# The sort's column one-hots in two-byte form, with their numbers laid down in pairs

## The reference, cut to what matters

```python
h = relu(layernorm(x))
support = h @ weight
h1 = segment_sum(edge_weight[:, None] * support[dst], src)   # sums over the edges, by src
h2 = segment_sum(edge_weight[:, None] * h1[dst], src)        # the same again
x = x + relu(hop_w[0] * h1 + hop_w[1] * h2 + h)
h = relu(layernorm(x))
agg = segment_sum(h[src], dst)                               # sums by dst
x = x + mlp((1 + eps) * h + agg)                             # 4 layers, batch norm and elu between
```

## Time and profile before

| | |
|---|---|
| median of 3 runs | 4513.52 us (4511.48 to 4515.73) |
| the profiled execution: time | 4512.35 us |
| the profiled execution: span of its instructions | 4510.5 us |
| start and end of the move (first L1313, end of the last L1826) | 251.04 and 495.62 us |
| PE busy in the span | 3317.1 us (74%) |
| POOL busy in the span | 2678.9 us (59%) |
| DVE busy in the span | 1936.4 us (43%) |
| ACT busy in the span | 796.7 us (18%) |

### The profile page before, as it was taken

The page is one execution under the profiler, slowest core; times in us unless marked ns, Lnnn a source line. Parts: engine busy times, 40 slices in busy tenths (PEclk is TensorE's granted clock), DMA queues, the critical chain, the costliest instruction groups (busy, mean ns, idle before and its releaser), DMA issues. The chain is left out here.

```text
span 4510.5 us, 50631 instructions
## 1 busy us (share of the span) xinstructions
PE 3317.1 (74%) x15857; PEld 2707.2 (60%) x15857; DVE 1936.4 (43%) x4586; ACT 796.7 (18%) x1968; POOL 2678.9 (59%) x2705
## 2 busy tenths in 40 slices
PE   6759677777777767777777774566666665998998
PEld 5158555555555556665665564555555555887887
DVE  7989533333333323333333331222222224556765
ACT  4059300000000000000000000000000001545656
POOL 0068677777777767777777775777777775001000
PEclk9679899999999999999999997788888887999999
DMA  4000133333333343333333334433333333223313
GB/s 140 1 2 6 51 110 109 110 114 109 109 109 113 109 95 109 110 110 113 110 110 109 112 109 115 134 105 104 105 105 104 105 105 89 94 93 127 101 60 114
DMA packets 187133, 443.82 MB, mean 98 GB/s; under 512 B 49102, under 2 KB 96514, under 8 KB 180714
## 3 DMA queue, kind: packets, MB, share of 16 engines
q0 software_dynamic: 126464, 336.63, 26.0%
q1 hardware_dynamic: 60501, 105.26, 6.8%
HBM read 382.22 MB, written 59.49 MB: 98 GB/s over the span
## 5 line engine op out<-in xcount | busy, mean ns | idle before, releaser
L1859 PE MATMUL ps<-work 128*128 128x256 f32 x6912 | 1624.9, 389 | 574.5 <-DMA work<-table_hop,idx 574.5
L771 POOL DMA_INDIRECT work<-table_hop,idx x1728 | 1651.5, 956 | 556.6 <-issue 521.8
L1859 PEld LDWEIGHTS ps<-work 128*128 128x128 f32 x6912 | 1295.6, 192 | 901.9 <-DMA work<-table_hop,idx 486.6
L816 POOL DMA_INDIRECT work<-table_gin,idx x832 | 790.8, 950 | 282.3 <-issue 228.3
L1934 PE MATMUL ps<-work 128*128 128x128 f32 x3328 | 574.0, 344 | 409.1 <-DMA work<-table_gin,idx 378.0
L1934 PEld LDWEIGHTS ps<-work 128*128 128x128 f32 x3328 | 528.5, 250 | 479.0 <-DMA work<-table_gin,idx 314.3
L1399 DVE TENSOR_SCALAR work<-iota,w_hi,edge_buf 128x256 f32<-128x256 bf16 x1728 | 580.8, 408 | 18.7 <-issue 17.5
L1512 DVE TENSOR_TENSOR sum_b<-sum_b,ps 128x256 f32 x104 | 43.9, 422 | 800.3 <-PE ps L1934 800.3
L922 ACT COPY idx<-w 128x8 int32 (+1 forms) x216 | 42.1, 197 | 1947.7 <-PE ps L1859 1907.1
L1411 DVE TENSOR_TENSOR sum_b<-sum_b,ps 128x512 f32 x108 | 74.2, 687 | 718.6 <-PE ps L1859 718.6
L1411 DVE TENSOR_TENSOR big<-big,ps 128x512 f32 x108 | 74.3, 688 | 690.0 <-PE ps L1859 690.0
(11 more groups left out here) (220 smaller groups left out, 2678.7 us busy)
## 6 DMA issues: line engine op xcount, KB each, us to landing
work<-table_hop,idx POOLq DMA_INDIRECT x1728
z_dram<-sum_b SPq DMA_DIRECT2D x24, 1024.0 KB, 3.9
sum_b<-z_dram SPq DMA_DIRECT2D x24, 1024.0 KB, 5.1
work<-table_gin,idx POOLq DMA_INDIRECT x832
big<-x SPq DMA_DIRECT2D x12, 512.0 KB, 6.0
table_hop<-work SPq DMA_DIRECT2D x12, 512.0 KB, 2.9
table_hop<-sum_b SPq DMA_DIRECT2D x12, 512.0 KB, 3.3
x_dram<-big SPq DMA_DIRECT2D x12, 512.0 KB, 3.4
```

The costliest lines, as they stand in the source:

```text
L771: pool.indirect_dma_start(hop_rows[:, par, t, :], None, table[n], bass.IndirectOffsetOnAxis(idx[:, k % HR, t:t + 1], 0)).then_inc(rows_in[ ...
L816: pool.indirect_dma_start(rows[:, par, t, :], None, table[2], bass.IndirectOffsetOnAxis(idx[:, q, t:t + 1], 0)).then_inc(rows_in[par][half ...
L1859: mm = pe.matmul(ps[:, HWIN * par + b, 0:D], hot[:, par, t, b * P:(b + 1) * P], hop_rows[:, par, t, :], start=(t == 0), stop=(t == GT - 1))
```

## The change: what it does

The slot numbers are laid down as bf16, each twice in a row (`slot_twice`, 832 pairs in the buffer `w1`, where `slot_f` lay as f32), by the same conversion from integers as before with twice the elements. `hot_slot` becomes bf16, in the same place of the buffer `work`. The comparison is written with the 56 columns as 28 pairs: the innermost dimension now has two elements, over which the output, the column numbers and the slot numbers all step by one; the 28 repetitions of a pair of slot numbers are the dimension outside it. The slot numbers (up to 55), the column numbers and the values 0 and 1 are exact in bf16.

```diff
-        w1_all, w1_r, _ = both("w1", K1 * H1)
+        w1_all, w1_r, w1_h = both("w1", K1 * H1)
...
-        slot_f = w1_all[:, 0:TILES]
+        slot_twice = w1_h[:, 0:2 * TILES].rearrange("p (t u) -> p t u", u=2)
...
-        hot_slot = place(2 * BATCH * BCOLS).rearrange("p (s t w) -> p s t w", s=2, t=BATCH)
+        hot_slot = work_h[:, 2 * at[0]:2 * at[0] + 2 * BATCH * BCOLS].rearrange("p (s t w) -> p s t w", s=2, t=BATCH)
+        place(2 * BATCH * BCOLS)
...
-            chain(dve.tensor_copy(slot_f, scratch[3]))
+            chain(dve.tensor_copy(slot_twice, scratch[3].unsqueeze(2).to_broadcast([P, TILES, 2])))
...
-                at_ = [P, BATCH, BCOLS]
-                dve.tensor_tensor(hot_slot[:, par], iota[:, 0:BCOLS].unsqueeze(1).to_broadcast(at_),
-                                  slot_f[:, cols].unsqueeze(2).to_broadcast(at_), ALU.is_equal).then_inc(slot_hot, 1)
+                at_ = [P, BATCH, BCOLS // 2, 2]
+                columns = iota[:, 0:BCOLS].rearrange("p (w u) -> p w u", u=2).unsqueeze(1).to_broadcast(at_)
+                dve.tensor_tensor(hot_slot[:, par].rearrange("p t (w u) -> p t w u", u=2), columns,
+                                  slot_twice[:, cols, :].unsqueeze(2).to_broadcast(at_), ALU.is_equal).then_inc(slot_hot, 1)
```

## The result

| | before | after |
|---|---|---|
| median of 6 runs each | 4514.62 us (4511.48 to 4519.56) | 4486.05 us (4482.53 to 4492.07) |
| ratio, 95% interval | | 0.9937, 0.9924 to 0.9950 |
| profiled execution: time, span | 4512.35, 4510.5 us | 4485.54, 4483.7 us |
| the move: first `hot_slot` to end of the last matmul | 251.04 to 495.62 us | 252.09 to 468.14 us |

The kernel is 0.63% faster: 26.8 us of span, 28.6 us of median, where 27 were forecast. Lines of the changed kernel lie one or two further down: L1313 is now L1315, L1318 is L1320, L1322 is L1324, L901 is L902, L1826 is L1828, L738 is L739.

The account below looks back on a forecast made before the run. DVE was taken to set the move's pace, with ACT and PE close behind; 10.2 (pace) + 17.2 (hole) - 0.4 (conversion) = 27.0 us off 4512.35 gave 4485 us, range 4479 to 4506.

Parts of the forecast that it names:

- The comparison: L1313 in the move, 64 times: from 910 to 540 ns, saving 0.37 us per batch of DVE's pace.
- The conversion: L1288, once: twice the elements, from 584 ns to 1.02 us, a loss of 0.4 us.
- The pace: Steady batches of the move: from 3.45 to about 3.28 us each, 10.2 us over some 60 batches.
- The loop that was named: ACT and PE waiting on each other in the move: 3.215 us per batch, plus 0.06 for ACT's copy.
- The hole: Stall in the move around the first bin-storing DMA, 47.82 us long: its cost of 17.2 us would go.
- the first DMA needs more than one turn, each joint gives it little: Reading of the 47.82 us DMA: joints between DVE instructions hardly serve it; new DVE gaps finish it by about 298.
- A fixed time of the first DMA: Within the rival that the hole stays (chance 0.25): the DMA always takes 47.82 us, giving 4505 us.
- POOL loses a joint per batch: Rival, chance 0.06: in the move POOL misses one of two DMA turns per batch, costing 40 us, 4552.

Follow-up runs that it names:

- e1: The changed kernel with each slot number laid down once as bf16 and read with a step of 0, instead of in pairs; 4514.62 us, ratio to before 0.9998.
- e7: The changed kernel with three buffers of `load` instead of two, ACT waiting for the matmuls of batch k-3 instead of k-2; 4487.06 us.
- e11: e7 with `hot_slot` of batch k+1 made between `hot_part` and the product of batch k; 4484.92 us.
- e12: e11 with ACT's copy of a bin placed one batch later; 4481.49 us, ratio to before 0.9929.
- e3: The kernel before, with DVE's `hot_part` of batch 3 waiting for the matmuls of batch 2 instead of batch 1; 4498.08 us.
- e4: The kernel before, with DVE's `hot_part` of batch 7 waiting for the matmuls of batch 6 instead of batch 5; 4498.18 us.
- e2: The changed kernel with one more DVE instruction, an addition of 286 f32 numbers, behind each batch; 4523.05 us.
- e5: The kernel before, with POOL's memset of the hop sums moved behind the 112 stores of the move; 4514.31 us, ratio 1.0000.
- e6: The kernel before, with an indirect DMA of the same size added near the start of the program and waited for; 4524.72 us, ratio 1.0023.
- e8: The kernel before, with the first 600 columns of POOL's memset done right ahead of the move's first DMA; 4516.74 us.
- e9: The kernel before, with the first 2400 columns of POOL's memset done right ahead of the move's first DMA; 4519.35 us.
- e10: The kernel before, with the first 4600 columns of POOL's memset done right ahead of the move's first DMA; 4516.31 us.

## Why the prediction was right

**The comparison.** 540 ns forecast, 529 measured. That the fast rate of the one-input row holds for two inputs was the open bound, and the lower end was right. By the Trainium skill (VectorE: DVE Perf Modes, the perf-mode tier table) the estimate was 535; the trace agrees with it. In e1 one element read again and again stays at 908 ns, as the Trainium skill has it (Vector Engine (DVE) Microarchitecture Reference, section 5.1). Two elements per row are enough for the fast rate, as the changed kernel's 529 ns show.

**The conversion.** 1.02 us forecast, 1.020 measured. L1324 and L902 did not change, as assumed.

**The pace.** 3.28 forecast, 3.275 measured, with DVE's gaps where they were said to be. The loop that was named (ACT and PE over two buffers of `load`, 3.215 and the copy) is in the rows: ACT starts with PE's end, PE with ACT's. But it is not alone. e7 takes it away, and 3.24 remains. A second loop can be read from its rows: PE's end of batch k-2, `hot_part` 1.80, the product 0.83, `hot_slot` 0.53, ACT 3.13, PE 3.13, over three batches, which with the gaps is 3.22 per batch. e11 shortens it and gains nothing, with the copy's wait of 0.70 us in its place; e12 takes that away and gains 0.04, and its rows show the loop over `hot_part`, 3.215, behind it. The prediction had the number; for the belief that only one loop stood there it had no ground. A kernel whose next limits lie within 0.06 us of each other gives little for any one edit.

**The hole.** 17.2 us forecast to go, and it went. e3 and e4 price it alone at 17.1 to 17.2. The move by itself got 28.5 us shorter (244.57 to 216.05), so 11.3 are left for the pace (10.2 forecast). It also began 1.05 us later, 0.44 of it by the conversion; the start of the move lies between 249.8 and 252.9 in the traces here, so the rest says nothing. With 0.7 us more behind the move this gives the 26.8 us of span. That waits of DVE make the difference is shown: with the gaps closed the hole comes back (e1, e2), with one wait made longer in the kernel before it goes (e3, e4).

The reading behind it was wrong in one point, the step "the first DMA needs more than one turn, each joint gives it little". In the changed kernel the first DMA ends at 274.55, ahead of the first gap behind its start (274.82 to 275.12); so one joint was enough, and the gaps behind the DMA's start, which the forecast counted on, were not needed. In e4 such a gap does end the long DMA; but that the hole went in the changed kernel came about in another way than was forecast, and in this the number was lucky. A gap ahead went with a short DMA as well: in the changed kernel the last gap that the rows name ended 4.3 us before the DMA (268.51; the `hot_part` at 271.65 also started some 0.05 us late), in e11 4.2 us, in e3 1.2 us. In the eight traces with the long DMA (before, e1, e2, e5, e6, e8, e9, e10) DVE had run for 11.1 to 14.6 us without a gap when the DMA came; in each the DMA ended 0.9 to 1.0 us after DVE stopped, whether that was 44 or 48 us later, and in e4 after 7. Later DMAs pass at joints, even after 145 us without a gap, as the first one of the last bin in the kernel before:

```profile
482.18 1.89 DVE L1318 TENSOR_TENSOR work<-iota,edge_buf 128x1664 f32<-128x1664 bf16 x1
...
482.38 2.52 POOL L738 DMA_INDIRECT sorted_edges<-work  x1 [0.94 <-ACT work L892]
```

What the move's first one lacks stays open. The memset, first use and a memset of POOL right ahead were ruled out. Two rivals of the gap were not separated from it. One is the instant. The long DMAs began 0.73 to 0.86 us into a `hot_part`, or 0.56 into a product (e9); those that passed with no gap in the 11 us ahead all began 0.2 or 1.2 us into a `hot_part`, or inside a `hot_slot`; and in the changed kernel, e3, e7 and e11 the first DMA began 1.15 to 1.16 us into one, where ACT's copy, which the DMA waits for, had started together with that `hot_part` (both at 271.65 above); in e12 it began 0.1 us into one. Only e4 has a DMA that began like the long ones, at 0.83, and met a gap: it ended in it. The other rival is POOL's own last DMA: each later DMA began at most 1.9 us behind the end of another, while the first had none before it, or one some 259 us earlier (e6). How long a stretch without a gap it would take, between 4.2 and 11.1 us, was not tried. The rule of the Trainium skill that the prediction weighed (SBUF — State Buffer, the two separate sides: the loser waits for the end of the holder's instruction) fits the later DMAs, and not the first one of the move in these eight traces.

**The rivals.** A fixed time of the first DMA is refuted by e4 and e10. That POOL loses a joint per batch did not happen: from 271.65 to 284.75 POOL issued all seven DMAs of a bin and then waited for ACT (25.1 us of such waits in the move, none of ACT for POOL).

## What to carry to other kernels

Before an engine is called the bound, add up the loops that run through its neighbours and their buffers: here DVE was shortened by 0.37 us per batch, 0.18 showed (3.45 to 3.275), and each further step (e7, e11, e12) gave 0.04 at most. And look for single long instructions of POOL beside a DVE that never rests: here short waits of DVE, 0.2 to 0.3 us each, went with the loss of a 17 us hole, more than the 11 us of the better pace.

## What had not been expected of the hardware

The move's first indirect DMA of POOL, where DVE had been busy without a gap for 11 us or more, waited until DVE stopped: 44 to 48 us in eight traces, over some 40 ends of DVE instructions. Behind a gap of 0.25 us, 4.3 us earlier, the same DMA took 1.74 us. Later DMAs passed within 2.6 us in those same traces, with or without gaps.

The gathers of the hops took 946 or 947 ns in the median in most kernels, but 949 in e2 and 957 in e6 (one indirect DMA more, at the start of the program); the two hops took 3.4 and 13.7 us longer there. No run tells why.
